# Expert biases of the sorted tiles: from bias products on TensorE to additions on VectorE and GpSimd

## The chip, the cores and the metric

The kernel is a whole decoder of two layers, run as one program on one NeuronCore of one Trainium2 chip. The metric is the device time of one execution, in microseconds, as the median of the runs; smaller is better. 64 sequences of 64 tokens with 256 features are computed, 4096 tokens in all.

## The reference, cut to what matters

The change concerns the expert layer of layer 0 and, by way of a shared buffer, two biases of layer 1.

```python
def _L0_ffn_ref(hidden_states, router_weight, router_bias, gate_up_proj, gate_up_proj_bias, down_proj, down_proj_bias):
    ALPHA = 1.702; LIMIT = 7.0; TOP_K = 2
    E, H, I = (8, 256, 256)
    h = hidden_states.reshape(-1, hidden)
    logits = h @ router_weight.T + router_bias
    top_vals, top_idx = jax.lax.top_k(logits, TOP_K)
    top_w = jax.nn.softmax(top_vals, axis=-1)
    ...
    gate_up = jnp.einsum('th,ehj->etj', h, gate_up_proj) + gate_up_proj_bias[:, None, :]
    gate = gate_up[..., ::2]
    up = gate_up[..., 1::2]
    gate = jnp.minimum(gate, LIMIT)
    up = jnp.clip(up, -LIMIT, LIMIT)
    glu = gate * jax.nn.sigmoid(gate * ALPHA)
    act = (up + 1.0) * glu
    expert_out = jnp.einsum('eti,eih->eth', act, down_proj) + down_proj_bias[:, None, :]
    out = jnp.einsum('te,eth->th', scores, expert_out)
```

Each token uses the two best of eight experts, so 8192 token rows are computed and not 8 x 4096.

## The kernel before, in words

`decoder` (line 2336) calls three stages one behind the other: `linear_attention` (line 82, layer 0's attention), `recurrence_and_experts` (line 785) and `layer_one` (line 1543). Each engine has its own list of instructions in each stage and waits by semaphores; nothing reorders a list while it runs. A list says `wait_ge(S("name"), n)`, and the instruction that makes the data says `then_inc(S("name"), 1)`.

The middle stage first runs the recurrence over the blocks of the sequence and the router in pipelined steps (`BLOCKS` = 8 blocks of 512 tokens). In its beginning SP loads the small tables, the first context blocks and the biases: `b_in` (line 885) takes all three bias tables into SBUF, GpSimd doubles the down bias and splits all of them into three bf16 pieces (lines 960 to 970), SP writes the pieces to the DRAM tensor `bias_rows` in nine small transfers (line 893), and reads them back as `bkv` (line 896, for the cross attention of layer 1), `bgu` and `bdn` (lines 899, 900), between which the gate and up weights (`wgu`, 4 MB, line 897) and the down weights (`wd_low`, 2 MB, line 898) stand. ScalarE stores keys and values of the context block by block; its instruction of line 1236 makes `m_kvs`, which SP writes to `context_kv`. The weights are split in a high and a low fp32r part; the high part of the down weights, `wd_high`, is copied by ScalarE behind its last router step (line 1277), and the low part is made by GpSimd (line 1029).

Behind the recurrence, VectorE makes the tile table: the token rows are sorted by expert and cut into `SLOT_TILES` = 72 tiles (`N`) of 128 rows, each of one expert; `who_i` holds the expert of each tile. Then comes the **tile loop**, the last part of the middle stage. For tile i:

- SP `load(i)` (line 929) reads 128 rows into `hs` (four buffers, `LOADS`), and `store(i)` (line 933) writes `ys` (two buffers, `STORES`) to DRAM, `LAG` = 7 steps behind the loads.
- TensorE `rows_T` (line 1138) transposes the rows to PSUM `HT` (in the trace `m_TV`); ScalarE copies them to the high part of `hT` (line 1286), and VectorE makes the low part, bank less high part (`low`, line 1505).
- TensorE `gate_up` first multiplies three rows of ones with the bias's three bf16 pieces (line 1146, `ones3` x `bgu`), then adds six fp32r products of 128x128 by 512 (line 1149), all into PSUM `GU` (`m_TK`). The gate and up product together are 512 columns.
- VectorE `gate_and_up` reads the bank twice: `gp` is the gate limited to 7 (line 1518), `ur` the up part limited to -7..7 (line 1519). ScalarE makes tanh of `gp` (line 1292), which gives the sigmoid with a factor of two. VectorE `product` makes the gated unit in `th` (line 1523), then `ac`, the activation (line 1529).
- TensorE `act_T` (line 1158) transposes `ac` to `AT` (`m_TF`), ScalarE copies it to `aT` (line 1298), VectorE makes its low part (line 1505).
- TensorE `down` multiplies the ones with the bias pieces `bdn` (line 1167), and adds six products with `wd_high` and `wd_low` (line 1170), into `YB` (`m_TY`). ScalarE evicts it to `ys` (`y_out`, line 1304).
- Which expert's weights a product takes is an address register; `chosen` (line 1175) loads it from `who_i` on TensorE's sequencer.

GpSimd does nothing in this loop. HT, GU, AT and YB have two buffers each, one for even and one for odd tiles. The order of the lists was written by hand. In round i, TensorE runs `rows_T(i+3)`, `gate_up(i+2)`, `chosen(i+3)`, `act_T(i+1)`, `down(i)`; ScalarE `hT_out(i+3)`, `aT_out(i+1)`, `tanh(i+2)`, `y_out(i)`; VectorE `gate_and_up(i+2)`, `low` of `hT` (i+3), `low` of `aT` (i+1), `product(i+2)`. So VectorE makes the low part of the next tile's rows, for which `gate_up` waits (`x_hTl`), behind the clamps of the tile before.

## Time and profile before

| | us |
|---|---|
| median of 3 runs | 3142.83 |
| lowest, highest | 3130.08, 3142.85 |
| span of the profiled execution | 3137.3 |
| TensorE busy over the span | 2826.3 (90%) |
| VectorE busy | 2581.5 (82%) |
| ScalarE busy | 1949.5 (62%) |
| GpSimd busy | 2038.0 (65%) |

The profile is one execution, and its times are microseconds from the start of the span. PE is TensorE, PEld its weight loads, which overlap the products, DVE VectorE, ACT ScalarE, POOL GpSimd, SP the engine that issues the transfers. `PEq` or `PEldq` is TensorE's sequencer: register operations, which are not counted as busy. L1149 is line 1149 of the kernel. `x6` counts instructions; a time in brackets with an arrow is idle time ahead of an instruction and the work whose end released it. In the trace names have the stage in front: `m_TK` is `TK` of the middle stage. The busy shares are means over stages with different limits, and so the rows below are taken from single stretches.

The span's three stages: layer 0's attention to about 1481 us, recurrence and router from there, the tile loop from about 1745 to 2002 us, and layer 1 to the end.

### The profile page before, as it was taken

How to read it: one execution, taken by the hardware profiler on the slowest of the kernel's cores; microseconds unless marked ns; L12 is line 12 of the kernel's file. 1: busy time of each engine (PE TensorE's matmuls, PEld its weight loads, DVE VectorE, ACT ScalarE, POOL GpSimd, SP SyncE). 2: the span in 40 equal slices, each digit the busy share in tenths (PEclk: the TensorE clock that was granted, in tenths of full speed). 3: DMA queues.
4: the chain of work that ended last, by engine and by line, in shares of the span. 5: the costliest groups of instructions: out<-in, count | busy, mean ns of one | idle time of the engine just before them, and what ended most of it. 6: DMA issues, size and time to landing. Idle time of an engine off the chain costs nothing. (4 is left out here: it accounts for less than half of the span.)

```text
span 3137.3 us, 68808 instructions
## 1 busy us (share of the span) xinstructions
PE 2826.3 (90%) x21864; PEld 2304.6 (73%) x21864; DVE 2581.5 (82%) x5745; ACT 1949.5 (62%) x4213; POOL 2038.0 (65%) x2535
## 2 busy tenths in 40 slices
PE   6999999999999999997786799657899999999978
PEld 3888888888888888886454577435777777777767
DVE  6888888888888888886597566478999999999973
ACT  5888877787877778785343333245565656565632
POOL 5886666666666666665487200178888888888870
PEclk8999999999999999998897899767999999999999
DMA  4564444444444444442422222300000000000000
GB/s 145 168 206 158 134 145 136 141 141 145 135 147 128 140 134 138 154 130 82 160 103 74 85 77 77 124 14 18 20 20 25 20 25 20 25 18 27 15 9 11
DMA packets 178643, 288.05 MB, mean 92 GB/s; under 512 B 42255, under 2 KB 103832, under 8 KB 177707
## 3 DMA queue, kind: packets, MB, share of 16 engines
q1 hardware_dynamic: 172206, 267.46, 25.8%
q0 software_dynamic: 6144, 16.79, 1.7%
q8 instruction: 171, 2.80, 0.3%
q14 instruction: 122, 1.00, 0.1%
HBM read 221.99 MB, written 53.78 MB: 88 GB/s over the span
## 5 line engine op out<-in xcount | busy, mean ns | idle before, releaser
L1740 POOL TENSOR_TENSOR l_prod<-l_sco,l_kv 128x256 f32<-128x256 f32 x512 | 380.0, 781 | 47.5 <-DVE l_sco L2254 47.5
L1733 POOL TENSOR_TENSOR l_prod<-l_q,l_kv 128x256 f32<-128x256 f32 x512 | 358.6, 740 | 62.1 <-DVE l_att L2262 62.1
L717 DVE SCALAR_TENSOR_TENSOR a_cq<-a_PQ,a_taps,a_cq 128x504 f32<-128x504 f32 (+2 forms) x384 | 281.7, 734 | 74.0 <-ACT a_cq L583 64.9
L717 DVE SCALAR_TENSOR_TENSOR a_ck<-a_PK,a_taps,a_ck 128x504 f32<-128x504 f32 (+2 forms) x384 | 280.6, 731 | 9.7 <-ACT a_ck L583 0.6
L341 POOL TENSOR_TENSOR a_tq<-a_cq,a_tq 128x512 f32<-128x512 f32 x128 | 165.5, 1293 | 131.3 <-ACT a_tq L589 131.2
L328 POOL TENSOR_TENSOR a_hrs<-a_hve,a_neghalf 128x8 f32<-128x8 f32 x128 | 209.4, 1636 | 25.9 <-DVE a_hve L734 25.4
L484 PE MATMUL a_Y<-a_wo,a_og_parts 128*128 128x256 f32 x1536 | 206.2, 284 | 4.2 <-POOL a_og_parts L335 4.2
L411 PEld LDWEIGHTS a_X<-a_wv,a_xb 128*128 128x128 f32 x1536 | 199.9, 188 | 12.1 <-issue 1.2
L411 PE MATMUL a_PQ<-a_x_hi,a_wqk 128*128 (+1 forms) x512 | 195.3, 422 | 12.0 <-issue 11.3
L341 POOL TENSOR_TENSOR a_tk<-a_ck,a_tk 128x512 f32<-128x512 f32 x128 | 163.3, 1276 | 64.1 <-ACT a_tk L589 64.1
L411 PE MATMUL a_X<-a_wv,a_xb 128*128 128x256 f32 x1536 | 204.2, 282 | 0.8 <-DMA a_xb<-a_x_lo 0.8
L484 PEld LDWEIGHTS a_Y<-a_wo,a_og_parts 128*128 128x128 f32 x1536 | 195.1, 192 | 5.5 <-issue 5.4
L602 ACT ACTIVATE a_hk<-a_PK,a_lncol 128x512 f32<-128x512 f32 x128 | 99.9, 781 | 154.5 <-PE a_PK L503 154.5
L596 ACT ACTIVATE a_nq<-a_TQ,a_hnb,a_hrs 128x128 f32<-128x128 f32 x512 | 191.6, 460 | 1.5 <-POOL a_hnb L331 1.0
L596 ACT ACTIVATE a_nk<-a_TK,a_hnb,a_hrs 128x128 f32<-128x128 f32 x512 | 191.1, 457 | 0.0
L411 PE MATMUL a_X<-a_x_hi,a_wg 128*128 (+1 forms) x512 | 184.3, 400 | 2.3 <-DVE a_og L742 2.3
L411 PE MATMUL a_PK<-a_x_hi,a_wqk 128*128 (+1 forms) x512 | 182.6, 397 | 0.0
L335 POOL TENSOR_TENSOR a_og_parts<-a_og,a_og_parts 128x512 fp32r<-128x512 f32 x128 | 166.1, 1298 | 19.9 <-ACT a_og_parts L609 19.9
L1712 POOL MEMSET l_cmask<- 128x512 bf16 x1 | 0.5, 524 | 255.4 <-POOLq L2354 255.4
L583 ACT ACTIVATE a_cq<-a_PQ,a_taps 128x512 f32<-128x512 f32 x128 | 99.8, 779 | 101.3 <-PE a_PQ L411 101.3
L771 DVE TENSOR_TENSOR_SCAN a_em<-a_dr,a_dm 128x256 f32<-128x256 f32 x128 | 159.7, 1247 | 0.0
L2262 DVE TENSOR_REDUCE l_att<-l_prod 128x64 f32<-128x1024 f32 x128 | 151.7, 1206 | 8.6 <-POOL l_prod L1740 8.3
(403 smaller groups left out, 8534.5 us busy)
## 6 DMA issues: line engine op xcount, KB each, us to landing
a_wqk<-qk_parts SPq DMA_DIRECT2D x112, 512.0 KB, 3.3
a_wv<-v_parts SPq DMA_DIRECT2D x56, 512.0 KB, 3.7
a_wg<-g_parts SPq DMA_DIRECT2D x112, 256.0 KB, 3.1
a_wo<-o_parts SPq DMA_DIRECT2D x112, 256.0 KB, 2.8
a_dr<-decays SPq DMA_DIRECT2D x256, 64.0 KB, 2.6
m_hs<-sorted_rows SPq DMA_DIRECT2D x72, 128.0 KB, 2.0
sorted_outs<-m_ys SPq DMA_DIRECT2D x72, 128.0 KB, 1.7
qk_parts<-a_wqk SPq DMA_DIRECT2D x16, 512.0 KB, 3.3
```

Of the source, the lines that this page charges most:

```text
L328: nc.gpsimd.tensor_tensor(out=hrs[q][:], in0=hve[q][:], in1=neghalf[:], op=ALU.pow).then_inc(s_hrstd, 1)
L335: nc.gpsimd.tensor_tensor(out=og_parts[q][:, 1, :], in0=og[q][:], in1=og_parts[q][:, 0, :].bitcast(F32), op=ALU.subtract).then_inc(og_lo, 1)
L341: nc.gpsimd.tensor_tensor(out=t[i][p][:], in0=c[i][p][:], in1=t[i][p][:], op=ALU.mult).then_inc(s_silu, 1)
L411: last = nc.tensor.matmul(out, lhs(i, k), rhs(j, k), start=at_pass == PASSES[0], stop=at_pass == PASSES[-1])
L484: last = nc.tensor.matmul(Y[:, j, :], og_parts[p][:, i, j * P:(j + 1) * P], wo[p][:, w, :], start=first and j % 2 == 0 and k == 0, stop=Tr ...
L596: nc.scalar.activation(nrm[i][q][:, j, :], TB[i][:, j, :], ACT.Identity, bias=hnb[q][:, k:k + 1], scale=hrs[q][:, k:k + 1]).then_inc(s_nor ...
L602: nc.scalar.activation(hat[i][q][:], PB[i][:], ACT.Identity, bias=lncol[:, 2 * i + 1:2 * i + 2], scale=lncol[:, 2 * i:2 * i + 1]).then_inc ...
L717: nc.vector.scalar_tensor_tensor(out=acc, in0=src, scalar=taps[p][:, tap + k:tap + k + 1], in1=acc, op0=ALU.mult, op1=ALU.add).then_inc(s_ ...
L771: nc.vector.tensor_tensor_scan(out=flat(em[q]), data0=flat(dr[q]), data1=flat(dm[q]), initial=0.0, op0=ALU.mult, op1=ALU.add).then_inc(s_e ...
L1733: nc.gpsimd.tensor_tensor(out=prod[:, h], in0=qv[:, h:h + 1, :].to_broadcast([P, H, HD]), in1=kk, op=ALU.mult).then_inc(S("E_pqk"), 1)
L1740: nc.gpsimd.tensor_tensor(out=prod[:, h], in0=sco[:, h:h + 1, :].to_broadcast([P, HD, H]), in1=vv, op=ALU.mult).then_inc(S("E_pav"), 1)
L2262: nc.vector.reduce_sum(att[:].rearrange("p (h d) -> p h d", d=HD)[:, 4 * k:4 * k + 4, :], prod[:, 4 * k:4 * k + 4], axis=AX).then_inc(S("E ...
```

## The change

**TensorE** no longer multiplies ones with bias pieces: `gate_up` and `down` consist of their six products, of which the first starts the sum. The gate product runs a tile further ahead: round i now has `rows_T(i+4)`, `gate_up(i+3)`, `act_T(i+1)`, `down(i)`, and ScalarE's and VectorE's lists move with it.

**VectorE**, in `gate_and_up`, loads the tile's expert in an address register, waits for the product, and adds PSUM `GU` and the expert's row of `b_gu_rows` into SBUF `gu` (two buffers). The two clamps read `gu`. `GU` is free for TensorE behind the addition (`x_bias`) and no longer behind the clamps.

**GpSimd** has a loop of its own: for each tile it loads the expert, waits for ScalarE's eviction (now `x_ye`), adds the expert's row of `b_down_rows` to `ys` in place, and lets SP store it (`x_y`). TensorE's `down` waits for the eviction. There are four `ys` buffers, and the stores run nine steps behind the loads.

**The bias rows** are broadcast to all 128 partitions by the transfer: the down bias (`b_down_rows`, 1 MB) at the front of the stage behind the weights, doubled by ScalarE after step 0 (`b_down2`), the gate and up bias (`b_gu_rows`, 2 MB) behind the last block of the recurrence, in whose buffers it lies. The pieces in DRAM remain for the other biases alone: three transfers in place of nine, and one small load in place of three, `bgu` and `bdn` are not read back.

**The high part of the down weights** shares its memory with other buffers than before, and its copies wait for the last block's `den`, `num`, `y`, `yT`, `pscan` and `qscan`.

```diff
-        b_in, b_rest = sb("b_in", [P, 56]), sb("b_rest", [P, 56])
-        b_piece = some(3, "b_piece", [P, 56], BF16)
+        b_in, b_rest = sb("b_in", [P, 8]), sb("b_rest", [P, 8])
+        b_piece = some(3, "b_piece", [P, 8], BF16)
         wkv, bkv, kvs = sb("wkv", [P, DC, 2 * D]), sb("bkv", [3, 2 * D], BF16), some(2, "kvs", [P, 2 * D])
-        bgu, bdn, ones3 = sb("bgu", [3, E, I2], BF16), sb("bdn", [3, E, D], BF16), sb("ones3", [3, P], BF16)
+        b_down_rows, ones3 = sb("b_down_rows", [P, E, D]), sb("ones3", [3, P], BF16)
...
-            wd_high, hs = own("wd_high", [P, E, DC, D], F32R), own_some(4, "hs", [P, D])
+            b_gu_rows, wd_high = own("b_gu_rows", [P, E, I2]), own("wd_high", [P, E, DC, D], F32R)
+            hs = own_some(4, "hs", [P, D])
+            gp, th, ur, ac = (own_some(2, n, [P, D]) for n in ("gp", "th", "ur", "ac"))
+            gu = own_some(2, "gu", [P, I2])
+            aT, ys = own_some(2, "aT", [P, 2, DC, P], F32R), own_some(4, "ys", [P, D])
...
-            gp, th, ur, ac = (own_some(2, n, [P, D]) for n in ("gp", "th", "ur", "ac"))
-            aT, ys = own_some(2, "aT", [P, 2, DC, P], F32R), own_some(2, "ys", [P, D])
...
-            LOADS, STORES, LAG = 4, 2, 7
+            LOADS, STORES, LAG = 4, 4, 9
...
+                sp.dma_start(b_in[:], b_cross).then_inc(S("b_in"), 16)
                 sp.dma_start(wkv[:], w_kv).then_inc(S("kv_w"), 16)
                 sp.dma_start(ctx_t[1][:], ctx_in[BLK:2 * BLK, :].rearrange("(j p) d -> p j d", p=P)).then_inc(S("ctx_in1"), 16)
-                sp.wait_ge(S("b_split"), 6)
-                at = 0
-                for cols in (slice(0, 32), slice(32, 48), slice(48, 56)):
-                    n = (cols.stop - cols.start) * P
-                    for q in range(3):
-                        sp.dma_start(bias_rows[q, at:at + n].rearrange("(p c) -> p c", p=P), b_piece[q][:, cols]).then_inc(S("b_out"), 16)
...
-                sp.wait_ge(S("b_out"), 16 * 9)
-                sp.dma_start(bkv[:], bias_rows[:, E * 3 * D:E * 3 * D + 2 * D]).then_inc(S("kv_w"), 16)
+                sp.wait_ge(S("b_split"), 5)
+                for q in range(3):
+                    sp.dma_start(bias_rows[q, :].rearrange("(p c) -> p c", p=P), b_piece[q][:]).then_inc(S("b_out"), 16)
+                sp.wait_ge(S("b_out"), 16 * 3)
+                sp.dma_start(bkv[:], bias_rows[:, 0:2 * D]).then_inc(S("kv_w"), 16)
...
-                sp.dma_start(bgu[:].rearrange("q e c -> q (e c)"), bias_rows[:, 0:E * I2]).then_inc(S("experts_in"), 16)
-                sp.dma_start(bdn[:].rearrange("q e c -> q (e c)"), bias_rows[:, E * I2:E * 3 * D]).then_inc(S("experts_in"), 16)
+                sp.dma_start(b_down_rows[:].rearrange("p e c -> p (e c)"), b_down.to_broadcast([P, E * D])).then_inc(S("b_down_in"), 16)
...
+                for done, n in (("vT", BLOCKS), ("fT", BLOCKS), ("kvp", BT * BLOCKS), ("fv", BLOCKS), ("ev", BLOCKS)):
+                    sp.wait_ge(S(done), n)
+                sp.dma_start(b_gu_rows[:].rearrange("p e c -> p (e c)"), b_gu.to_broadcast([P, E * I2])).then_inc(S("b_gu_in"), 16)
...
-                pool.wait_ge(S("b_in"), 48)
-                nc.gpsimd.tensor_tensor(out=b_in[:, 32:48], in0=b_in[:, 32:48], in1=b_in[:, 32:48], op=ALU.add).then_inc(S("b_split"), 1)
+                pool.wait_ge(S("b_in"), 16)
+                nc.gpsimd.tensor_copy(b_piece[0][:], b_in[:]).then_inc(S("b_split"), 1)
                 pool.wait_ge(S("b_split"), 1)
-                nc.gpsimd.tensor_copy(b_piece[0][:], b_in[:]).then_inc(S("b_split"), 1)
...
+                pool.wait_ge(S("table"), 15)
+                pool.wait_ge(S("b_down2"), 1)
+                for i in range(N):
+                    e = bass.ds(nc.gpsimd.value_load(who_i[0:1, i:i + 1], min_val=0, max_val=E - 1), 1)
+                    pool.wait_ge(S("x_ye"), i + 1)
+                    nc.gpsimd.tensor_tensor(out=ys[i % STORES][:], in0=ys[i % STORES][:], in1=b_down_rows[:, e, :].rearrange("p e c -> p (e c)"),
+                                            op=ALU.add).then_inc(S("x_y"), 1)
...
                     if i >= 2:
-                        pe.wait_ge(S("x_gp"), i - 1)
-                        pe.wait_ge(S("x_ur"), i - 1)
-                    nc.tensor.matmul(GU[i % 2], ones3[:], bgu[:, e, :].rearrange("q e c -> q (e c)"), start=True, stop=False)
+                        pe.wait_ge(S("x_bias"), i - 1)
                     for c in range(DC):
                         for k, m in PARTS:
-                            last = nc.tensor.matmul(GU[i % 2], hT[i % 2][:, k, c, :], wgu[:, m, e, c, :].rearrange("p e c -> p (e c)"), start=False,
-                                                    stop=c == DC - 1 and (k, m) == PARTS[-1])
+                            last = nc.tensor.matmul(GU[i % 2], hT[i % 2][:, k, c, :], wgu[:, m, e, c, :].rearrange("p e c -> p (e c)"),
+                                                    start=c == 0 and (k, m) == PARTS[0], stop=c == DC - 1 and (k, m) == PARTS[-1])
...
-                        pe.wait_ge(S("x_y"), i - 1)
-                    nc.tensor.matmul(YB[i % 2][:, 0:D], ones3[:], bdn[:, e, :].rearrange("q e c -> q (e c)"), start=True, stop=False)
+                        pe.wait_ge(S("x_ye"), i - 1)
                     for c in range(DC):
                         for k, m in PARTS:
                             last = nc.tensor.matmul(YB[i % 2][:, 0:D], aT[i % 2][:, k, c, :], (wd_high, wd_low)[m][:, e, c, :].rearrange("p e c -> p (e c)"),
-                                                    start=False, stop=c == DC - 1 and (k, m) == PARTS[-1])
+                                                    start=c == 0 and (k, m) == PARTS[0], stop=c == DC - 1 and (k, m) == PARTS[-1])
                     last.then_inc(S("x_dn"), 1)
...
-                pe.wait_ge(S("experts_in"), 64)
+                pe.wait_ge(S("experts_in"), 32)
...
-                for i in range(-3, N):
-                    if i + 3 < N:
-                        rows_T(i + 3)
-                    if 0 <= i + 2 < N:
-                        gate_up(i + 2, expert[i + 2])
-                        if i + 3 < N:
-                            expert[i + 3] = chosen(i + 3)
+                for i in range(-4, N):
+                    if i + 4 < N:
+                        rows_T(i + 4)
+                    if 0 <= i + 3 < N:
+                        gate_up(i + 3, expert[i + 3])
+                        if i + 4 < N:
+                            expert[i + 4] = chosen(i + 4)
                     if 0 <= i + 1 < N:
                         act_T(i + 1)
                     if i >= 0:
@@ -1267,17 +1269,15 @@
                     if r is not None:
...
+                    if f == 0:
+                        act.wait_ge(S("b_down_in"), 16)
+                        nc.scalar.activation(b_down_rows[:], b_down_rows[:], ACT.Copy, scale=2.0).then_inc(S("b_down2"), 1)
+
+                for done in ("den", "num", "y", "yT", "pscan", "qscan"):
+                    act.wait_ge(S(done), BLOCKS)
+                for n in range(4):
                     experts = slice(n * E // 4, (n + 1) * E // 4)
                     nc.scalar.activation(wd_high[:, experts], wd_low[:, experts].bitcast(F32), ACT.Copy).then_inc(S("wd_high"), 1)
-
-                for done in ("den", "num", "y", "yT", "pscan"):
-                    act.wait_ge(S(done), BLOCKS)
...
-                    nc.scalar.activation(ys[i % STORES][:], YB[i % 2][:, 0:D], ACT.Copy).then_inc(S("x_y"), 1)
-
-                for i in range(-3, N):
-                    if i + 3 < N:
-                        hT_out(i + 3)
+                    nc.scalar.activation(ys[i % STORES][:], YB[i % 2][:, 0:D], ACT.Copy).then_inc(S("x_ye"), 1)
...
+                for i in range(-4, N):
+                    if i + 4 < N:
+                        hT_out(i + 4)
                     if 0 <= i + 1 < N:
                         aT_out(i + 1)
-                    if 0 <= i + 2 < N:
-                        tanh(i + 2)
+                    if 0 <= i + 3 < N:
+                        tanh(i + 3)
...
+                        dve.wait_ge(S("b_gu_in"), 16)
+                    e = bass.ds(nc.vector.value_load(who_i[0:1, i:i + 1], min_val=0, max_val=E - 1), 1)
                     dve.wait_ge(S("x_gu"), i + 1)
+                    if i >= 2:
+                        dve.wait_ge(S("x_gp"), i - 1)
+                        dve.wait_ge(S("x_ur"), i - 1)
+                    nc.vector.tensor_tensor(out=gu[i % 2][:], in0=GU[i % 2], in1=b_gu_rows[:, e, :].rearrange("p e c -> p (e c)"),
+                                            op=ALU.add).then_inc(S("x_bias"), 1)
+                    dve.wait_ge(S("x_bias"), i + 1)
                     if i >= 2:
                         dve.wait_ge(S("x_th"), i - 1)
                         dve.wait_ge(S("x_gl"), i - 1)
                         dve.wait_ge(S("x_ac"), i - 1)
-                    nc.vector.tensor_scalar(gp[i % 2][:], GU[i % 2][:, 0:D], LIMIT, None, ALU.min).then_inc(S("x_gp"), 1)
-                    nc.vector.tensor_scalar(ur[i % 2][:], GU[i % 2][:, D:I2], LIMIT, -LIMIT, ALU.min, ALU.max).then_inc(S("x_ur"), 1)
+                    nc.vector.tensor_scalar(gp[i % 2][:], gu[i % 2][:, 0:D], LIMIT, None, ALU.min).then_inc(S("x_gp"), 1)
+                    nc.vector.tensor_scalar(ur[i % 2][:], gu[i % 2][:, D:I2], LIMIT, -LIMIT, ALU.min, ALU.max).then_inc(S("x_ur"), 1)
...
-                for i in range(-3, N):
-                    if 0 <= i + 2 < N:
-                        gate_and_up(i + 2)
-                    if i + 3 < N:
-                        low(i + 3, hT, HT, "x_hTe", "x_hTl")
+                for i in range(-4, N):
+                    if 0 <= i + 3 < N:
+                        gate_and_up(i + 3)
+                    if i + 4 < N:
+                        low(i + 4, hT, HT, "x_hTe", "x_hTl")
                     if 0 <= i + 1 < N:
                         low(i + 1, aT, AT, "x_aTe", "x_aTl")
-                    if 0 <= i + 2 < N:
-                        product(i + 2)
+                    if 0 <= i + 3 < N:
+                        product(i + 3)
...
+        bias_rows = nc.dram_tensor("bias_rows", (3, 4 * D), BF16, kind="Internal").ap()
...
-        "b_gu": np.concatenate([gub[:, 0::2], gub[:, 1::2]], axis=1).reshape(P, -1), "b_down": i["L0_ffn_down_proj_bias"].reshape(P, -1),
+        "b_gu": np.concatenate([gub[:, 0::2], gub[:, 1::2]], axis=1).reshape(1, -1), "b_down": i["L0_ffn_down_proj_bias"].reshape(1, -1),
```

## Rows read from the trace of the kernel before

**Rows 1.** Stretches: us, busy (xcount) of PE, PEld, DVE, ACT, POOL; clock, DMA, GB/s
```profile
1555.00:1565.00 10.00, 8.56 (x43) 4.22 (x43) 9.33 (x42) 3.18 (x6) 4.67 (x5) 1.00 0.28 105
1800.00:1900.00 100.00, 100.00 (x522) 71.38 (x522) 62.66 (x174) 38.90 (x116) 0.00 (x0) 1.00 0.24 77
```
**Rows 2.** Order of time in one tile: start, duration (us), engine, line, operation
```profile
1863.28 0.39 PE L1146 MATMUL m_TK<-m_bgu,m_ones 3*128 x1
1863.59 1.66 PE L1149 MATMUL m_TK<-m_wgu,m_hT 128*128 x6
...
1865.08 0.38 PE L1158 MATMUL m_TF<-ident,m_ac 128*128 128x128 f32 x2
1865.28 0.42 DVE L1518 TENSOR_SCALAR m_gp<-m_TK 128x256 f32<-128x256 f32 x1 [1.15 <-PE m_TK L1149]
1865.40 0.28 PE L1167 MATMUL m_TY<-m_bdn,m_ones 3*128 x1
...
1865.60 0.39 PE L1170 MATMUL m_TY<-m_wd_high,m_aT 128*128 x1
...
1865.78 0.41 ACT L1292 ACTIVATE m_th<-m_gp 128x256 f32<-128x256 f32 x1
...
1865.95 0.41 DVE L1505 TENSOR_TENSOR m_hT<-m_TV,m_hT 128x256 fp32r<-128x256 f32 x1
...
1866.42 0.38 PE L1138 MATMUL m_TV<-ident,m_hs 128*128 128x128 f32 x2
...
1866.62 0.41 DVE L1523 SCALAR_TENSOR_TENSOR m_th<-m_th,m_gp 128x256 f32<-128x256 f32 x1
1866.74 0.39 PE L1146 MATMUL m_TK<-m_bgu,m_ones 3*128 x1
...
1867.16 0.42 DVE L1529 SCALAR_TENSOR_TENSOR m_ac<-m_ur,m_th 128x256 f32<-128x256 f32 x1
```
**Rows 3.** Table of waits, 1740 to 2002 us: idle us, times, longest
```profile
DVE m_gp L1518 <- PE m_TK L1149: 86.9, 72, 3.8
...
PE m_TK L1146 <- DVE m_hT L1505: 1.4, 2, 0.9
```
**Rows 4.** Order of time while the tile loop fills
```profile
1755.48 0.41 DVE L1505 TENSOR_TENSOR m_hT<-m_TV,m_hT 128x256 fp32r<-128x256 f32 x1
...
1756.03 0.38 PE L1146 MATMUL m_TK<-m_bgu,m_ones 3*128 x1 [0.41 <-DVE m_hT L1505]
```
**Rows 5.** Groups by line of VectorE, all stages: count | busy us, mean ns | idle before
```profile
L764 DVE TENSOR_TENSOR a_tg<-a_tg,a_X 128x512 f32<-128x512 f32 x128 | 88.0, 688 | 24.3 <-ACT a_tg L638 17.8
...
L1471 DVE TENSOR_SCALAR m_keep<-m_keep,m_wc 128x512 f32<-128x512 f32 x2 | 0.9, 480 | 0.0
...
L1448 DVE TENSOR_SCALAR m_who<-m_who 128x72 f32<-128x72 f32 x1 | 0.2, 198 | 0.0
```
**Rows 6.** Lines 1175, 1146 on TensorE's sequencer: ns min/median/max, first to last start
```profile
L1175 PEldq TENSOR_LOAD <-m_who_i x72: 296/301/491, 1739.5 to 1991.7; - x72
L1175 PEldq FUSED_REGOPS  x72: 151/151/165, 1740.0 to 1992.1; - x72
...
L1146 PEldq FUSED_REGOPS  x72: 46/46/56, 1746.4 to 1994.4; - x72
```
**Rows 7.** Instructions of lines 683, 2190 and 1740: ns min/median/max, first to last start
```profile
L683 DVE TENSOR_SCALAR a_nq<-x_sb,a_mv,a_rs x16: 402/410/2433, 11.0 to 43.9; 128x256 f32<-128x256 f32 x16
...
L2190 DVE TENSOR_TENSOR l_qkt<-l_qr,l_rt x32: 425/944/958, 2025.1 to 2962.0; 128x256 f32<-128x256 f32 x32
...
L1740 POOL TENSOR_TENSOR l_prod<-l_sco,l_kv x512: 709/730/977, 2079.2 to 3061.5; 128x256 f32<-128x256 f32 x171
```
**Rows 8.** Stage's front: SP's issues in order, ScalarE's wait, a stretch (columns as above)
```profile
1488.54 4.13 SPq L893 DMA_DIRECT2D bias_rows<-m_b_piece  x9
...
ACT m_kvs L1236 <- DMA context_kv<-m_kvs: 13.6, 1, 13.6
...
1505.00:1510.00 5.00, 3.48 (x8) 0.96 (x6) 5.00 (x1) 0.00 (x0) 4.21 (x2) 1.00 0.95 403
```

More of the change, by code:

```diff
@@ L958, in _ @@
                                         channel_multiplier=-1).then_inc(S("const"), 1)
-                pool.wait_ge(S("b_in"), 48)
-                nc.gpsimd.tensor_tensor(out=b_in[:, 32:48], in0=b_in[:, 32:48], in1=b_in[:, 32:48], op=ALU.add).then_inc(S("b_split"), 1)
+                pool.wait_ge(S("b_in"), 16)
+                nc.gpsimd.tensor_copy(b_piece[0][:], b_in[:]).then_inc(S("b_split"), 1)
                 pool.wait_ge(S("b_split"), 1)
-                nc.gpsimd.tensor_copy(b_piece[0][:], b_in[:]).then_inc(S("b_split"), 1)
+                nc.gpsimd.tensor_tensor(out=b_rest[:], in0=b_in[:], in1=b_piece[0][:], op=ALU.subtract).then_inc(S("b_split"), 1)
                 pool.wait_ge(S("b_split"), 2)
-                nc.gpsimd.tensor_tensor(out=b_rest[:], in0=b_in[:], in1=b_piece[0][:], op=ALU.subtract).then_inc(S("b_split"), 1)
+                nc.gpsimd.tensor_copy(b_piece[1][:], b_rest[:]).then_inc(S("b_split"), 1)
                 pool.wait_ge(S("b_split"), 3)
-                nc.gpsimd.tensor_copy(b_piece[1][:], b_rest[:]).then_inc(S("b_split"), 1)
+                nc.gpsimd.tensor_tensor(out=b_rest[:], in0=b_rest[:], in1=b_piece[1][:], op=ALU.subtract).then_inc(S("b_split"), 1)
                 pool.wait_ge(S("b_split"), 4)
-                nc.gpsimd.tensor_tensor(out=b_rest[:], in0=b_rest[:], in1=b_piece[1][:], op=ALU.subtract).then_inc(S("b_split"), 1)
-                pool.wait_ge(S("b_split"), 5)
                 nc.gpsimd.tensor_copy(b_piece[2][:], b_rest[:]).then_inc(S("b_split"), 1)
@@ L1269, in _ @@
                         weights_high(r)
-                for n, (read, count) in enumerate((("vT", BLOCKS), ("vT", BLOCKS), ("fT", BLOCKS), ("kvp", BT * BLOCKS))):
-                    act.wait_ge(S(read), count)
-                    if n == 3:
-                        act.wait_ge(S("fv"), BLOCKS)
-                        act.wait_ge(S("ev"), BLOCKS)
+                    if f == 0:
[4 more added lines that the diff above has]
+                for n in range(4):
                     experts = slice(n * E // 4, (n + 1) * E // 4)
                     nc.scalar.activation(wd_high[:, experts], wd_low[:, experts].bitcast(F32), ACT.Copy).then_inc(S("wd_high"), 1)
-                for done in ("den", "num", "y", "yT", "pscan"):
-                    act.wait_ge(S(done), BLOCKS)
                 def hT_out(i):
@@ L1692, in _ @@
                 sp.dma_start(tensor[:], a[name]).then_inc(S("w_in"), 16)
-            at = 8 * 3 * D + 2 * D
+            at = 2 * D
             for tensor in (ebq3, ebo3):
@@ L2366, in decoder @@
         outs = nc.dram_tensor("sorted_outs", ((2 * TILES + 8) * P, D), F32, kind="Internal").ap()
-        bias_rows = nc.dram_tensor("bias_rows", (3, 8 * 3 * D + 4 * D), BF16, kind="Internal").ap()
+        bias_rows = nc.dram_tensor("bias_rows", (3, 4 * D), BF16, kind="Internal").ap()
         kvd = nc.dram_tensor("context_kv", (TOK, 2 * D), F32, kind="Internal").ap()
```

3 lines of the change are left out of this document (removed).

## The prediction

> **What bounds the kernel now.** The change lives in one stage of a long program, so I first found that stage's times, then its period, then what ends last in the period. The view by stretches shows the tile stage running flat: from 1800 to 1900 us TensorE is busy all the time, at the full granted clock, VectorE 63%, ScalarE 39%, GpSimd not at all [rows 1]. The order of time then gives one tile: the bias product of the gate starts at 1863.28 and again at 1866.74, a period of 3.46 us, 72 of them [rows 2]. Inside it TensorE's starts follow each other without a hole: 0.31 us from the gate's bias product to the first gate product, 1.49 us to the transposes, 0.32 to the bias product of the down projection, 0.20 to the down products, 0.82 to the next transposes, 0.32 to the next bias product; the sum is 3.46. The table of waits agrees from the other side: VectorE waits for the gate product in all 72 tiles, TensorE for VectorE in two only [rows 3]. So TensorE sets the period.
>
> The reader should also look for the second-longest loop, since it takes over when TensorE gets shorter. A gate product needs its transposed rows' low part, which VectorE makes right behind its work on the gate product before. The loop is bare for a moment while the stage fills: the low part starts at 1755.48, ends at 1755.89, and TensorE, which had waited 0.41 us for it, starts at 1756.03, 0.14 later [rows 4]. In the steady state the loop is: 0.14 wake-up, 0.31 bias product, 1.66 gate products to their end, 0.03 to VectorE, 0.67 for the two clamps (1865.28 to 1865.95), 0.41 low part [rows 2, 4]: 3.22 us. It has only 0.24 us to spare against 3.46.
>
> **The change part by part.**
> *The two bias products go.* TensorE's own work falls by 0.31 + 0.20 = 0.51 to 2.95 us a tile [rows 2]. If TensorE stayed the bound that would be worth 0.51 x 70 tiles = 36 us (I count 70 periods; the ends come below).
>
> *VectorE adds the gate and up bias, inside the loop.* The add is 128x512 with one operand in PSUM; the same form in layer 0 takes 0.69 us [rows 5]. The first clamp waits for it: a dependent pair on VectorE shows 0.13 us between end and start (1866.62 + 0.41 to 1867.16 [rows 2]); here the other waits can pass during the add, so between 0 and 0.13, and I take 0.08, nearer that pair. The add's bias row is picked by a register, and before TensorE's such instruction stands a register operation of 0.046 us that starts the address [rows 6]; on VectorE it would stand behind the wait for the gate product. No row shows it there: 0 to 0.15, I take 0.10, from the 0.14 wake-up of rows 4, which includes one.
>
> *The clamps read SBUF instead of PSUM.* They take 0.335 each now. For SBUF to SBUF there are two rows: 72 columns take 0.198 and 512 columns take 0.480 (that one with a per-partition scalar) [rows 5]. Through both, 256 columns come to 0.198 + 184 x 0.282/440 = 0.32, and as instructions here overlap by 0.08 (0.335 start to start against a duration of 0.41 to 0.42) a start-to-start of 0.20 to 0.24; I take 0.22, with 0.34 (no gain) as the other end.
> The 512-column row itself says that two columns pass per cycle. The Trainium skill (VectorE: DVE Perf Modes, The perf-mode tier table) says the same: fp32 scalar operations between SBUF tensors run at twice the rate that any PSUM operand allows, and a two-tensor add does not. The rows agree; by a rule without that gain the loop would be 0.24 us longer.
>
> *The loop afterwards*: 0.14 + 1.66 + 0.03 + 0.10 + 0.69 + 0.08 + 0.22 + 0.22 + 0.41 = 3.55 us. All unknowns low: 3.33; all high: 3.89. So the loop takes over from TensorE (2.95), and the period goes from 3.46 to 3.55: + 0.09 x 70 = +6 us. What is late next is the same VectorE chain; a tile more of lead does not help, because rows and gate move forward together and the low part still stands behind the clamps.
>
> *The gate product a tile further ahead.* It takes the wait for the activations off TensorE (now the product has a tile and more to finish), which covers the later clamps. Its cost is at the end: the last tile's chain is longer by the add, less the clamps' gain, about 0.6 us, and by GpSimd's add and its wake-up, about 0.8 us: +1.3 us. SP's loop moves with it: stores nine steps behind loads, four store buffers; SP issues a load and a store per tile and mostly waits, so 0.
>
> *The register reads.* VectorE and GpSimd read the tile's expert each tile. On TensorE this takes 0.30 + 0.15 + 0.02 us in the sequencer, while the array works [rows 6]. On VectorE it stands behind the product and before the wait for the next gate product, where VectorE has idled 1.15 us [rows 2]. The new chain there: product dispatched, 0.6 us of reading, 0.10 register operation. From the add: 0.77, clamps 0.44, two low parts 0.67, the two product steps 0.54, then 0.74: 3.16 us, under 3.55, so 0 unless something lengthens it (below).
>
> *GpSimd adds the down bias.* A 128x256 add takes 0.73 us [rows 7], on an engine idle here, 1 per 3.55 us: 0 by itself. The stores wait for it, and have a tile's time with four buffers.
>
> *The front of the stage.* SP issues two loads and six small stores fewer before the weights: nine of them take 4.13 us [rows 8], 0.46 each, so the 6 MB of weights start 8 x 0.46 = 3.7 us earlier. Behind them 1 MB of down bias is added; the queues there move 403 GB/s at a 0.95 share [rows 8], so 2.6 us. ScalarE's wait for the first stored block, 13.6 us long [rows 8], ends behind these bytes: 1.1 us sooner. The new wait of ScalarE for the down bias stands right before that one, with those stores and the rounds' loads queued behind it; as the bias is ahead of them in the queue it is covered by the 13.6 us, and so is the doubling. A broadcast row of 8 KB read 128 times is nowhere in the trace: -4 to +8 us, and I take -1. The gate-up bias (2 MB) is issued behind the last recurrence, where SP next waits for the whole tile table, and it is first read after that table, the rows' loads and a gate product: 0.
> *The copies of the down weights* now wait for the last recurrence; on ScalarE's list they stand behind the last router step, which itself comes after that recurrence: 0.
>
> **Sum.** +6.3 + 1.3 - 1.1 = +6.5. The profiled span is 3137.3, 5.5 under the median of 3142.83; the span becomes 3144, the time 3149 us.
>
> **The rivals.**
> *A, forecast: the loop through the clamps bounds.* Its own range, with the middle half of the unknowns (3.42 to 3.70) and the front: 3138 to 3160 us. For it: it is bare in rows 4, and every big term is a measured row. Chance 0.52.
>
> *B, slower: GpSimd's add holds up VectorE's product.* The trace has it twice. A scalar operation between SBUF tensors that takes 0.40 took 2.43 us beside a long GpSimd add, and a two-tensor operation between SBUF tensors that takes 0.425 alone has a median of 0.944 beside GpSimd's adds of 0.73 [rows 7]. In a tile, tanh follows the first clamp, the eviction follows tanh, GpSimd's add follows that: some 1.17 us behind the clamp's start; VectorE's first product step comes 0.44 + 0.67 = 1.11 behind it. They meet within 0.1 us. If VectorE is first, only the second step is held and the register read runs beneath it; if GpSimd is first, 0.52 to 0.73 go on the chain of 3.16: 3.68 to 3.89 us, over the loop's 3.55. It decides as soon as the hold-up is over 0.39. Price: (0.22 to 0.43) x 70 + 0.2 = 15.6 to 30 us, 3158 to 3173. Chance 0.26.
> The Trainium skill (SBUF - State Buffer, Who interferes with whom) has a rule for this: the two engines share one pair of ports, an instruction of VectorE with two SBUF inputs and one of GpSimd that reads SBUF exclude each other for a whole instruction, and whichever issues first wins. The rows agree with it, and by it case B costs a full 0.73.
>
> *C, slower: the clamps gain nothing* (0.34 each): loop 3.79, +23 us, 3166. Against it: the 480 ns row. Chance 0.06.
>
> *D, faster: TensorE stays the bound at 2.95*, -36 us, 3107, or the loop comes out near its low end and the front gains 4: 3125. It needs the low part not to wait for the clamps, and the order of VectorE's list says it does. Chance 0.08.
>
> *E: the front.* The broadcast reads are slow and ScalarE and the first rounds stand: +8 on A, 3157. Chance 0.05.
>
> *F: TensorE's clock.* With 0.6 us of waiting per tile the granted clock could fall to 1.2 GHz; from 1555 to 1565 us it is busy 86% and still granted 1.00 [rows 1]. Chance 0.03, beyond the range.
>
> **How the numbers follow.** The likeliest case gives 3149. The range takes in A's unknowns and B and C: 3131 to 3177; outside lie D's larger part, F and the tails. A measurement of this kernel tells about 0.5% (15.7 us) from no change. Slower by more than that: most of B and C, F, the high tail of A: 0.36. Faster by more: D: 0.08. Within: 0.56.
>
> **What would show it.** Right: 144 TensorE bias products gone; period near 3.55; TensorE waiting for VectorE's low part in nearly every tile, VectorE's clamps at 0.30, product steps at 0.41. B: product steps at 0.8 or more, VectorE without idle time before the add. C: clamps at 0.41. D: period near 2.95 and TensorE busy throughout. E: ScalarE's wait at the front over 14 us. I am wrong if the period leaves 3.33 to 3.89, or if time changes outside the front and the tile stage.

## The result

The kernel after takes 3155.85 us (median of 4), the one before 3140.94 on the same chip; the two medians are 14.9 us apart, and the ratio estimated from all runs is 1.0044, with a 95% interval of 1.0025 to 1.0064. Measured once more with more runs it is 1.0026 (1.0013 to 1.0039). What both intervals allow is +8 to +12 us: slower, by about what a measurement can tell. Forecast were +6.5 us and 3149.

The steady state first: the stretch that stood in [rows 1], the waits that answer to [rows 3], and one period in order of time, which answers to [rows 2].

After, 1800 to 1900 us (busy time and count of PE, PEld, DVE, ACT, POOL; clock, DMA share, GB/s):
```profile
1800.00:1900.00 100.00, 80.21 (x453) 64.82 (x454) 83.63 (x200) 38.47 (x115) 26.09 (x29) 1.00 0.25 75
```
After, table of waits over the tile loop (idle us, times, longest):
```profile
PE m_TK L1152 <- DVE m_hT L1505: 52.1, 71, 1.6
...
DVE m_gu L1519 <- PE m_TK L1152: 34.4, 72, 3.2
```
After, order of time:
```profile
1870.66 1.67 PE L1152 MATMUL m_TK<-m_wgu,m_hT 128*128 x6 [0.69 <-DVE m_hT L1505]
...
1870.76 0.41 DVE L1531 SCALAR_TENSOR_TENSOR m_th<-m_th,m_gp 128x256 f32<-128x256 f32 x1
1870.87 0.90 POOL L1034 TENSOR_TENSOR m_ys<-m_ys,m_b_down_rows 128x256 f32<-128x256 f32 x1 [2.60 <-ACT m_ys L1304]
1871.31 0.74 DVE L1537 SCALAR_TENSOR_TENSOR m_ac<-m_ur,m_th 128x256 f32<-128x256 f32 x1
...
1872.47 0.69 DVE L1519 TENSOR_TENSOR m_gu<-m_TK,m_b_gu_rows 128x512 f32<-128x512 f32 x1 [0.41 <-PE m_TK L1152]
...
1873.19 0.29 DVE L1526 TENSOR_SCALAR m_gp<-m_gu 128x256 f32<-128x256 f32 x1
1873.40 0.28 DVE L1527 TENSOR_SCALAR m_ur<-m_gu 128x256 f32<-128x256 f32 x1
...
1873.61 0.42 DVE L1505 TENSOR_TENSOR m_hT<-m_TV,m_hT 128x256 fp32r<-128x256 f32 x1
...
1874.16 1.66 PE L1152 MATMUL m_TK<-m_wgu,m_hT 128*128 x6 [0.69 <-DVE m_hT L1505]
```
TensorE was busy all the time and waited for VectorE in two tiles; now it is busy 80% of the time and waits some 0.7 us in 71 of 72. The period is the loop of the prediction, link by link: 1.81 us from the gate product to the addition, 0.72 to the first clamp, 0.21 and 0.21 for the clamps, 0.55 from the low part's start to the next gate product, together 3.50. The register operation is in the 1.81, and the wake-up in the 0.55.

Over the whole loop, one line of each kernel gives the period: the first and the last start of the gate's clamp, 71 periods apart. Before, then after:
```profile
L1518 DVE TENSOR_SCALAR m_gp<-m_TK x72: 423/424/425, 1750.1 to 1996.5; 128x256 f32<-128x256 f32 x72
```
```profile
L1526 DVE TENSOR_SCALAR m_gp<-m_gu x72: 293/294/295, 1753.8 to 2003.5; 128x256 f32<-128x256 f32 x72
```
These are 246.5 against 249.6 us (by the starts to two digits), 3.47 and 3.52 a tile. That is 3.1 us more, and the two traces differ by 9.8. From the 11th to the 61st tile the period goes from 3.46 to 3.52, which would be 4.1 us over the whole loop. But the trace of before needed 1.0 us more for its first ten tiles than for ten later ones. Its granted clock was 0.71 from 1750 to 1760 us, where that of after was 1.00 from 1753 to 1763. The place that nobody had priced is where the stage ends. After, order of time (a stage's first instruction on GpSimd is `l_cmask`):
```profile
2008.19 0.38 ACT L1304 ACTIVATE m_ys<-m_TY 128x256 f32<-128x256 f32 x1 [0.66 <-PE m_TY L1172]
...
2008.74 0.72 POOL L1034 TENSOR_TENSOR m_ys<-m_ys,m_b_down_rows 128x256 f32<-128x256 f32 x1 [0.32 <-ACT m_ys L1304]
...
2016.40 0.52 POOL L1720 MEMSET l_cmask<- 128x512 bf16 x1 [6.93 <-POOLq L2362]
```
GpSimd's sequencer at the end of the stage, after, then before (ns, start in us):
```profile
L852 POOLq DRAIN  x1: 6069/6069/6069, 2008.7 to 2008.7; - x1
```
```profile
L852 POOLq DRAIN  x1: 23666/23666/23666, 1731.1 to 1731.1; - x1
```
Before, the same place:
```profile
2001.28 0.38 ACT L1304 ACTIVATE m_ys<-m_TY 128x256 f32<-128x256 f32 x1 [0.72 <-PE m_TY L1170]
...
2004.85 0.52 POOL L1712 MEMSET l_cmask<- 128x512 bf16 x1 [255.37 <-POOLq L2354]
```
The time from the end of the last eviction to the start of the next stage is called the seam below. It was 2004.85 - 2001.66 = 3.19 us; now it is 2016.40 - 2008.57 = 7.83. GpSimd closes its list with an instruction called DRAIN. Before, GpSimd had no work in the tile loop, and the drain was over at 1754.8, long before the end; now it stands behind the last addition, and the other engines wait for it. SyncE, which waits for the last store, is through at 2011.5 and goes on at 2015.0, when the drain has ended (2014.8); so it is not the store that the stage waits for now. After:
```profile
L852 SPq DRAIN  x1: 7/7/7, 2011.5 to 2011.5; - x1
L852 SPq EVENT_SEMAPHORE  x1: 17/17/17, 2015.0 to 2015.0; - x1
```

### The profile page after: what moved, and what is told of

Read it like the earlier page. It is cut to its first block and busy times, and to the rows that moved or that the text cites. A ratio compares the mean times of both kernels' runs of the same rounds, so it can differ in the third digit from the quotient of the medians.

```text
span 3147.1 us, 69127 instructions
## 1 busy us (share of the span) xinstructions
PE 2776.0 (88%) x21688; PEld 2291.7 (73%) x21720; DVE 2635.0 (84%) x5817; ACT 1951.4 (62%) x4214; POOL 2101.6 (67%) x2606
## 3 DMA queue, kind: packets, MB, share of 16 engines
q1 hardware_dynamic: 171330, 270.51, 26.8%
## 5 line engine op out<-in xcount | busy, mean ns | idle before, releaser
L1034 POOL TENSOR_TENSOR m_ys<-m_ys,m_b_down_rows 128x256 f32<-128x256 f32 x72 | 64.1, 890 | 192.2 <-ACT m_ys L1304 192.2
L1152 PE MATMUL m_TK<-m_wgu,m_hT 128*128 x432 | 121.2, 416 | 52.1 <-DVE m_hT L1505 52.1
```

The costliest lines, as they stand in the source:

```text
L1152: last = nc.tensor.matmul(GU[i % 2], hT[i % 2][:, k, c, :], wgu[:, m, e, c, :].rearrange("p e c -> p (e c)"), start=c == 0 and (k, m) == P ...
```

## The experiments

Theory A is that of the prediction: the period is the loop gate product, addition, clamps, low part, next gate product. Theory B: VectorE's own list, with the register read and the second product that GpSimd holds up (0.74 us instead of 0.42), is what fills the period. The edits are shortened to the calls that moved, and words among them that are not code say where a call stood. Each ratio is to the kernel before, measured beside it on the same chip, with a 95% interval.

**One clamp out of the loop** (up_clamp_later).
```diff
 gate_and_up(i + 3): addition, gp
 low(i + 4, hT, ...)
+ur of i + 3
 low(i + 1, aT, ...)
-(ur was behind gp)
```


> The changed kernel with one move: VectorE's up clamp stands behind the low part of the next rows, no longer ahead of it. Theory A (the loop gate product, addition, clamps, low part, next gate product sets the period): one clamp of 0.21 us leaves the loop, the period falls from 3.50 to 3.29 us, about 15 us over 70 tiles. Theory B (VectorE's own list with the register read and the product step held up by GpSimd sets it): the list has the same instructions, the period stays at 3.50.


3133.37 us, a ratio of 0.9991 (0.9976 to 1.0007).
```profile
L1526 DVE TENSOR_SCALAR m_gp<-m_gu x72: 293/293/296, 1752.1 to 1988.6; 128x256 f32<-128x256 f32 x72
```
236.5 / 71 = 3.33 us a tile, 0.19 less than in the changed kernel, with the same instructions on VectorE's list. A holds, B falls.

**The whole low part ahead of the addition** (low_first).
```diff
-gate_and_up(i + 3); low(i + 4, hT, ...); low(i + 1, aT, ...); product(i + 3)
+e = chosen(i + 3); low(i + 4, hT, ...); gate_and_up(i + 3, e); low(i + 1, aT, ...); product(i + 3)
```


> The changed kernel with VectorE's low part of the next rows ahead of the addition of the gate bias (the register read stays ahead of both). Theory A: the loop is cut altogether, so the next bound decides: VectorE's list (0.72 addition, 0.42 clamps, 0.33 low part of the activations, 0.55 first product, 0.41 to 0.75 second product, 0.43 low part of the rows and the start of the addition) gives 2.9 to 3.2 us a tile against TensorE's 2.95; period 2.95 to 3.25, some 18 to 38 us less than the changed kernel. Theory B: the list stays as long as it is, 3.4 to 3.5.


3122.88 us, 0.9953 (0.9929 to 0.9977): faster than the kernel before. The gate's clamps give 3.18 us a tile.
```profile
L1530 DVE TENSOR_SCALAR m_gp<-m_gu x72: 293/295/297, 1747.9 to 1973.8; 128x256 f32<-128x256 f32 x72
```
```profile
L1541 DVE SCALAR_TENSOR_TENSOR m_ac<-m_ur,m_th x72: 425/878/890, 1749.2 to 1975.2; 128x256 f32<-128x256 f32 x72
```
With the loop cut, VectorE's list is the bound (it waits for a gate product in one tile only), and now GpSimd's hold-up costs: the second product takes 0.878 us.

**No addition on GpSimd** (no_down_bias).
```diff
-    (GpSimd's loop of 72 additions)
-ys <- YB, then_inc x_ye
+ys <- YB, then_inc x_y
```


> The changed kernel without GpSimd's loop: the down bias of the expert layer is left out, ScalarE's eviction goes straight to the store. Theory A: VectorE's second product step falls from 0.75 to 0.41 us but the period stays at 3.50, since 0.34 us of waiting stand ahead of the addition; the wait there grows by about 0.3. Theory B: the period falls by 0.2 to 0.3 us, 14 to 21 us. Seam: if GpSimd's closing drain of 6.07 us ends the stage in the changed kernel, the first instruction of the next stage comes about 5 us sooner after the last eviction (3.6 of the drain, 0.7 of the addition, 0.3 of the wake-up); if the last store ends the stage, about 1 us sooner.


This kernel leaves the down bias out. 3144.54 us, 1.0015 (1.0002 to 1.0028).
```profile
L1531 DVE SCALAR_TENSOR_TENSOR m_ac<-m_ur,m_th x72: 424/426/426, 1760.5 to 2013.5; 128x256 f32<-128x256 f32 x72
```
The second product is back at 0.426, and from the 21st to the 71st tile the period is 3.51, as without that edit: in the changed kernel the hold-up was covered. (The first three tiles of this trace ran at a granted clock of 0.50, the lower of its two levels, and its first ten tiles took 3.8 us more than in after.) The seam is 2020.08 - 2016.82 = 3.26 us.

**The drain.** Two runs, one that takes GpSimd's late work away and one that puts it into the kernel before.
```diff
 tail_on_vector:
-for i in range(N): GpSimd adds the down bias
+for i in range(N - 4): GpSimd adds the down bias; VectorE adds it for the last four tiles
 before_late_gpsimd:
+pool.wait_ge(S("x_y"), N)
+nc.gpsimd.memset(neghalf[:], -0.5).then_inc(S("late"), 1)
```


> The changed kernel with the down bias of the last four tiles added by VectorE, so that GpSimd's last instruction comes some 7 us sooner; nothing is left out. If GpSimd's drain (6.07 us from its last addition) ends the stage, the next stage starts 3 to 3.5 us sooner after the last eviction, the last store's landing ending the stage as it did before. If the drain waits for the end of the stage itself, whatever GpSimd did last, nothing moves. Period 3.50 by either.

> The kernel before with one instruction more: GpSimd waits for the last eviction of the tile loop and then writes a small constant again. If GpSimd's closing drain takes some 5 to 6 us from its last instruction whatever that was, the next stage starts 3 to 4 us later after the last eviction than the 3.19 us of the kernel before. If the drain of the changed kernel is long because of its 72 additions, nothing moves by more than 0.3 us.


tail_on_vector: 3148.88 us, 1.0024 (1.0007 to 1.0041), an interval too wide to show 3.5 us; the last eviction ends at 2007.61, the next stage starts at 2011.96: a seam of 4.35 us, VectorE's addition in it, 3.48 less than after. before_late_gpsimd, order of time and sequencer:
```profile
2004.63 0.38 ACT L1307 ACTIVATE m_ys<-m_TY 128x256 f32<-128x256 f32 x1 [0.73 <-PE m_TY L1173]
...
2005.07 0.10 POOL L1033 MEMSET m_neghalf<- 128x4 f32 x1 [250.67 <-ACT m_ys L1307]
2011.76 0.52 POOL L1715 MEMSET l_cmask<- 128x512 bf16 x1 [6.59 <-POOLq L2357]
```
```profile
L852 POOLq DRAIN  x1: 5441/5441/5441, 2005.1 to 2005.1; - x1
```
One write of 0.10 us makes the seam 6.75 instead of 3.19. The drain ends some 5.3 us behind GpSimd's last instruction, after one write as after 72 additions (2014.79 - 2009.46). The one run of before_late_gpsimd, 3152.17 us, says nothing on the total.

**The changed kernel again** (no edit).


> The changed kernel as it is, once more, for its distance from the kernel before. The sum read from the two traces (tile loop +3.2 us, chain of the last tile +0.9, seam behind the last eviction +3.7 beyond that, front of the stage -0.8; the rest in stages that the change doesn't touch) gives about +7 us, a ratio of 1.0022. If the 1.0044 of the first measurement holds, some 7 us are still unexplained.


3150.34 us, 1.0026. The clamps run from 1759.7 to 2008.9, 3.51 a tile, the seam is 7.83. This second reading is nearer to the +7 us of the sum.

**The lead undone** (lead_back).
```diff
-rows_T(i + 4); gate_up(i + 3); act_T(i + 1); down(i)      (ScalarE and VectorE alike)
+rows_T(i + 3); gate_up(i + 2); act_T(i + 1); down(i)
```


> The changed kernel with the old lead: rows three tiles and the gate product two tiles ahead, as before. By theory A the loop does not contain the lead, and the activations are ready about 0.2 us before TensorE comes to transpose them (addition 0.72, clamps 0.42, two low parts 0.66, products 0.55 and 0.75: 3.1 us behind the start of the addition, against 3.36 for the end of the next gate product): period 3.50 to 3.52, the chain at the end 0.5 to 1 us shorter. If the lead was what kept TensorE from waiting for the activations, the period rises to 3.6 or more.


3153.22 us, 1.0055 (1.0038 to 1.0072). Clamps from 1758.4 to 2007.7: 3.51 a tile, so the lead is worth nothing in the loop. The end, expected 0.5 to 1 us shorter, became longer: from the last clamp to the end of the last addition it is 6.66 us against 6.01, and why was not examined. The rest of the longer total does not lie in this stage: against the trace of after, layer 0 is 5.8 us longer and layer 1 4.6, and the edit touches neither.

**TensorE by itself.** Three runs of the kernel before: without its bias products (which leaves both biases out), the same with the low part first, and the low part first alone.
```diff
-matmul(GU, ones3, bgu), matmul(YB, ones3, bdn)            (before_no_bias, before_no_bias_low_first)
-gate_and_up(i + 2); low(i + 3, hT, ...)                   (before_low_first, before_no_bias_low_first)
+low(i + 3, hT, ...); gate_and_up(i + 2)
```


> The kernel before without its two bias products: both biases of the expert layer are left out, everything else stands. By the starts that the prediction took, TensorE's own work is 2.95 us a tile and the loop gate product, clamps on PSUM, low part is 3.22 - 0.31 = 2.91, so the period is 2.95 and TensorE does not wait. By the run with all three moves, TensorE can run in 2.74 us or less: then the loop is the bound, the period is 2.85 to 2.91, and TensorE waits for the low part in nearly every tile.

> The same without the biases, with VectorE's low part of the next rows ahead of the clamps, so that no loop of VectorE's stands behind a gate product: the period is TensorE's own work. 2.95 us if the prediction's subtraction was right, 2.65 to 2.74 if the two bias products cost TensorE 0.7 us and not 0.51.

> The kernel before with the low part of the next rows ahead of the clamps and nothing else. If TensorE sets its period, nothing moves: 3.46 us a tile, a ratio of 1.000. If VectorE's loop (3.22 by the sum) had a share in it, the period falls by up to 0.2 us, 14 us.


before_low_first: 3130.42 us, 0.9985 (0.9970 to 1.0001), 3.46 us a tile from the 11th to the 61st, as without the edit: TensorE did set the period. before_no_bias: 3097.13 us, 0.9892 (0.9873 to 0.9911), 2.91 us a tile from the 11th to the 61st; TensorE's weight load for the gate product sits idle 0.36 us in 70 of 72 tiles (`issue` means that the profile names no releaser):
```profile
PEld m_TK L1148 <- issue: 24.9, 70, 0.8
```
before_no_bias_low_first: 3069.71 us, 0.9788 (0.9768 to 0.9808), 1762.7 to 1942.2 for the clamps, 2.53 us a tile (2.54 from the 11th to the 61st), with TensorE busy for 100.00 of 100 us. So the low part was what before_no_bias waited for, and TensorE's own work is under both values that were expected, 2.95 and 2.65 to 2.74:
```profile
1871.08 0.38 PE L1157 MATMUL m_TF<-ident,m_ac 128*128 128x128 f32 x2
1871.22 0.36 PE L1168 MATMUL m_TY<-m_wd_high,m_aT 128*128 x1
...
1872.01 0.38 PE L1138 MATMUL m_TV<-ident,m_hs 128*128 128x128 f32 x2
1872.14 1.41 PE L1148 MATMUL m_TK<-m_wgu,m_hT 128*128 x5
```
**What is left on VectorE's list** (read_under_add, all_three).
```diff
 read_under_add: low_first, and
-chosen(i + 3) ahead of low(i + 4, hT, ...)
+chosen(i + 1) right behind the addition of i
 all_three: that, the last four tiles as in tail_on_vector, and on GpSimd
 pool.wait_ge(S("x_ye"), i + 1)
+pool.wait_ge(S("x_ac"), i + 4)
```


> As low_first (low part of the next rows ahead of the addition), and VectorE loads the next tile's expert right behind the addition's start and no longer behind the second product. In low_first the second product, held up to 0.88 us by GpSimd's addition, and the register read of 0.65 to 0.75 us run side by side. If the hold-up alone is enough to set that place, the period stays at 3.19 us; if the register read set it, the period falls by 0.1 to 0.3.

> The low part first, the register read under the addition, GpSimd's addition held until VectorE's second product is done (so that it runs beside VectorE's work on PSUM), and the down bias of the last four tiles on VectorE. Nothing is left out. If GpSimd's hold-up and the read are what is left on VectorE's list, that list is 2.7 to 2.8 us and TensorE's 2.95 us sets the period: 0.55 x 70 = 38 us less than the changed kernel in the loop and 3.5 us less at the seam. If reads of PSUM are held up by GpSimd as well, the period stays at 3.1 to 3.2.


read_under_add: 3122.81 us, 0.9933 (0.9912 to 0.9954); from the 11th to the 61st tile 3.18 us against 3.19 in low_first. So the register read does not set that place. In all_three GpSimd waits until VectorE's second product is done, which takes the hold-up away: 3090.89 us, 0.984 (0.982 to 0.9859).
```profile
1870.07 0.29 DVE L1533 TENSOR_SCALAR m_gp<-m_gu 128x256 f32<-128x256 f32 x1
...
1871.41 0.42 DVE L1544 SCALAR_TENSOR_TENSOR m_ac<-m_ur,m_th 128x256 f32<-128x256 f32 x1
...
1871.75 0.42 DVE L1506 TENSOR_TENSOR m_hT<-m_TV,m_hT 128x256 fp32r<-128x256 f32 x1
...
1872.07 0.73 POOL L1035 TENSOR_TENSOR m_ys<-m_ys,m_b_down_rows 128x256 f32<-128x256 f32 x1 [2.07 <-DVE m_ac L1544]
1872.09 0.68 DVE L1524 TENSOR_TENSOR m_gu<-m_TK,m_b_gu_rows 128x512 f32<-128x512 f32 x1
...
1872.80 0.29 DVE L1533 TENSOR_SCALAR m_gp<-m_gu 128x256 f32<-128x256 f32 x1
```
This is 2.73 us a tile (2.74 from the 11th to the 61st), under the 2.95 of TensorE that was expected to be the bound. VectorE waits for a gate product in one tile only, so its list is the bound. GpSimd's 0.73 us now lie beside VectorE's addition from PSUM, and that keeps its 0.68. This version is 50 us faster than the kernel before and 59 faster than after, both measured on the same chip.

## Why the prediction came out as it did

| part | forecast, us | measured |
|---|---|---|
| front of the stage, to the second block's `m_den` | -1.1 | -0.8 |
| router steps, to the tile loop | 0 | +2.8 |
| tile loop, first to last clamp | +6.3 | +3.1 (249.6 - 246.5) |
| last clamp to the last rows in `ys` | +1.3 | +0.9 (6.01 - 5.11) |
| from those rows to the next stage | 0 | +3.7 (6.93 - 3.19) |
| sum | +6.5 | +9.8 (before rounding) |

All lines come from the profiled pair, whose spans differ by 9.8 (`m_den` is a sum that VectorE forms for each block of the recurrence). Layer 0 is 1.7 longer and layer 1 1.7 shorter in that pair, though nothing was changed there. That the total came out near the forecast is in part luck: the loop cost 3.2 us less than forecast, and two places that were put at nothing cost 6.5 together.

**The direction and the mechanism were right.** TensorE set the period before (before_low_first), the loop through the clamps took over, the period came out at 3.50 to 3.52 where 3.55 was forecast, and a clamp moved out of the loop is worth 0.19 to 0.20 us a tile. (The middle half of 3.33 to 3.89 is 3.47 to 3.75 and not 3.42 to 3.70, as the prediction has it for rival A; nothing hangs on that.) The second-longest loop of the kernel before was put at 3.22; without the bias product's 0.31 that is 2.91, and before_no_bias ran at 2.91. The clamps from SBUF start 0.21 apart, as taken (0.22), so rival C falls. (That two columns pass per cycle can't be read from the 512-column row, since no row shows a cycle; what the traces show is 0.29 us from SBUF against 0.42 from PSUM for the same 256 columns.) From the addition to the clamp it took 0.72 where 0.77 was taken; that is the 0.05 between 3.50 and 3.55, since the other differences cancel. Rival F did not come either: the granted clock from 1800 to 1900 us is 1.00, with some 0.7 us of waiting in each tile.

**Where it was wrong: the seam.** "Its cost is at the end: ... +1.3" priced the last tile's chain, and stopped at the last store. What ends a stage on GpSimd was not asked, although the trace of before has such a drain, of 23.7 us and off the path. This is nearly all of the 3.7 us, as two runs show from both sides: without GpSimd's late work the next stage starts 3.28 us behind the last rows (tail_on_vector), and with one late write 6.75 us behind them (before_late_gpsimd). The prediction's own sign of being wrong was a time that changes outside the front and the tile stage. The router steps below are such a place, though it is not shown that the change is what moved them.

**TensorE's own work was mis-sized**: 2.95 forecast, 2.54 measured. The prediction subtracted the starts from each bias product to the next product, 0.31 and 0.20. But the starts ahead of the bias products were long too: in [rows 2] the transposes stand 0.32 us ahead of each; without bias products the next product comes 0.13 to 0.14 behind them. That makes 0.38 and 0.50, which is 0.88 of the 0.92 us a tile that the two cost (3.46 - 2.54, each from the 11th to the 61st tile). It did not touch the forecast, since the loop bounds, but it hid what the change gives away: of 0.92 x 70 = 64 us nothing is left.

**Rival B's place was right, its price was not due.** GpSimd's addition and VectorE's second product do meet in each tile, so the sign "product steps at 0.41" did not hold. VectorE's first product started 0.11 us ahead of GpSimd (1870.76 against 1870.87), which is the milder of the two cases that the prediction left open. The hold-up is 0.32 us (0.749 in the median against 0.426), under the 0.39 from which it would have counted, and the waiting ahead of the addition, 0.41 us in the tile shown and 0.48 in the mean, is what is left beside it. In low_first, without that cover, it costs 0.45 (0.878 against 0.426), and moving it away takes the period from 3.18 to 2.74 (11th to 61st tile). The Trainium skill (SBUF — State Buffer, Who interferes with whom) says that a VectorE instruction with two SBUF inputs contends with a GpSimd instruction that reads SBUF, and one with at most one SBUF input, outside the modes that use both of VectorE's port pairs, does not. The traces agree on both: 0.878 us for the second product in low_first, and 0.68 in all_three for the addition, whose other input is in PSUM (0.69 in after, where GpSimd doesn't run beside it).

**The lead** was said to take a wait off TensorE. There was none to take: lead_back has the same 3.51.

**The front** gave 0.6 of 1.1 us: between VectorE's additions of `m_den` for the first and the second block, five traces with the old front have 44.43 us in the mean and nine with the new one 43.79. (Counted from the stage's first instruction it is 63.85 and 63.42, or 0.4 us.) ScalarE waited 8.4 us for the down bias, doubled it in 1.9 and waited 3.0 more, in place of 13.6; rival E did not come.

**The router steps** were not in the forecast. In each trace two of their intervals (the fourth to the fifth and the fifth to the sixth `m_den`) take one of three lengths, about 24.1, 25.5 and 26.8 us. The first is at 26.7 or more in eight of nine traces with the new front, and in one of five with the old. TensorE's clock goes with it: in that interval the mean granted clock is 0.88 in all nine traces at 26.7 or more, 0.97 to 0.98 in the two at 25.5, and 1.00 in the three at 24.1 to 24.2. Near its start, before, then after:
```profile
1590.00:1600.00 10.00, 7.67 (x39) 5.94 (x40) 9.86 (x15) 5.17 (x10) 9.28 (x6) 0.83 0.30 105
```
```profile
1590.00:1600.00 10.00, 6.84 (x24) 5.00 (x24) 9.86 (x16) 4.56 (x8) 9.20 (x8) 0.66 0.30 105
```
Over all fourteen traces the way from the second to the last `m_den` takes 147.0 us in the mean with the old front (144.2 to 151.1) and 150.3 with the new (149.7 to 151.1). That the front makes the difference is not shown: no run changed it alone, one trace with the old front is as long as the longest with the new, and whether the length follows the clock or the clock the length stays open.

**From the span to the time.** The prediction set the profiled span of 3137.3 against the median and added 5.5. The spans and times of the kernel after stand 1.8 apart in each run (3147.1 and 3148.86 in the profiled one), those of before 2.2, so most of the 5.5 was the distance of one run from the median.

## What to carry to other kernels

When work leaves the bounding engine, look for the second-longest loop and put nothing into it; the instruction order around that loop can be worth as much as the work taken away (3.52 to 2.73 us a tile in all_three, with nothing left out). When an idle engine is given the last work of a stage, look at what it does when it closes its list. And to price an instruction's removal, take the starts on both sides of it, or a run without it.

## What the runs showed of the hardware

GpSimd's drain ends 5.3 us after the end of its last instruction in this stage in all fourteen traces, whether that was an addition of 0.72 us, a write of 0.10 or, in the kernel before, a low part of the down weights of 2.37 (it ends at 1749.47, the drain at 1754.80). At the end of the program it is 5.3 as well, at the end of layer 0 less than 0.1. GpSimd issues indirect transfers in those two stages and none in layer 0; whether that makes the difference was not tried. The two products of three rows cost TensorE 0.92 us a tile, against 2.54 for the twelve large products and four transposes around them. And the length of router steps in which nothing was changed came in levels some 1.35 us apart, with granted clocks of 1.00, 0.97 to 0.98, and 0.88.
